# Constants of VectorE's comparisons read from PSUM instead of SBUF, in three layers of a graph network

## The reference

```python
h = relu(layernorm(x)); x = x + L0(h)   # relational: sum over edges of h[src] @ weight[type], 16 types
h = relu(layernorm(x)); x = x + L1(h)   # mean: elu(mean over edges of h[src] @ W_l.T + b_l + h @ W_r.T)
h = relu(layernorm(x)); x = x + L2(h)   # message: m = silu([h[src], h[dst], edge_attr] @ w1 + b1) @ w2 + b2,
                                        #   agg = segment_sum(m, dst), update, layernorm
h = relu(layernorm(x)); x = x + L3(h)   # rule: attention with a softmax per destination and rule, 8 types
# the gather and the sum, as in L1:
msg = x[src]
agg = jax.ops.segment_sum(msg, dst, num_segments=n)
```

## Time and profile before

| | us |
|---|---|
| median of 3 runs | 2359.71 (2354.27 to 2363.16) |
| the profiled execution | 2357.4 |
| its span | 2355.6 |
| POOL busy | 1660.1 (70%) |
| PE busy | 1527.0 (65%) |
| DVE busy | 1062.7 (45%) |
| ACT busy | 486.8 (21%) |

### The profile page before, as it was taken

One profiled execution on the slowest core, in us unless ns is written; L12 is line 12 of the kernel. 1 busy time (PEld: TensorE's weight loads), 2 busy tenths in 40 slices (PEclk: granted clock), 3 DMA queues, 4 the chain that ended last, 5 costly groups with the idle time before them and its releaser, 6 DMA issues.

```text
span 2355.6 us, 28036 instructions
## 1 busy us (share of the span) xinstructions
PE 1527.0 (65%) x8443; PEld 1363.2 (58%) x8443; DVE 1062.7 (45%) x2213; ACT 486.8 (21%) x1153; POOL 1660.1 (70%) x1677
## 2 busy tenths in 40 slices
PE   7573333333588888764887777877858656657774
PEld 3243223322488888764777777777745436646673
DVE  6691111111587666643422222222255765455587
ACT  4000000000098676611100000000032121111120
POOL 5777777777388877872677777777517777777760
PEclk9775555555587777765755555555576886656677
DMA  8613131222111111110322232222217322323220
GB/s 280 205 28 94 24 95 32 68 41 50 25 35 40 35 36 39 38 23 10 79 58 57 58 62 59 57 58 57 44 52 254 84 72 80 77 63 86 68 68 14
DMA packets 159863, 159.27 MB, mean 68 GB/s; under 512 B 108361, under 2 KB 111993, under 8 KB 158748
## 3 DMA queue, kind: packets, MB, share of 16 engines
q0 software_dynamic: 48352, 68.42, 13.4%
q1 hardware_dynamic: 111372, 89.07, 13.3%
HBM read 118.71 MB, written 46.06 MB: 70 GB/s over the span
## 4 chain that ended last, share of the span: by engine, by line
POOL 67%; issue 19%; PE 6%; DVE 4%; DMA 4%; SPq 1%; ACT 0%; POOLq 0%; DVEq 0%; ACTq 0%
POOL flat L591 62%; POOL quiet L579 4%; DMA table<-flat 2%; PE ps L1404 1%; PE ps L1357 1%; PE ps L1657 1%; DMA flat<-table,flat 1%; PE ps L1332 1%; PE ps L1341 1%; PE ps L1601 0%; PE ps L1369 0%; DVE var L681 0%; DVE uvT L674 0%; DVE mean L672 0%; PE ps L1527 0%
## 5 line engine op out<-in xcount | busy, mean ns | idle before, releaser
L591 POOL DMA_INDIRECT flat<-table,flat x1061 | 1146.5, 1081 | 405.0 <-issue 289.1
L1404 PE MATMUL ps<-flat,oh 128*128 x1664 | 323.5, 375 | 393.4 <-DMA flat<-table,flat 367.5
L1404 PEld LDWEIGHTS ps<-flat,oh 128*128 128x128 f32 x1664 | 307.1, 285 | 420.0 <-issue 418.2
L801 DVE TENSOR_TENSOR oh<-iota_n,drel 128x1024 f32<-128x1024 f32 x156 | 190.9, 1224 | 624.7 <-PE ps L1404 424.7
L591 POOL DMA_INDIRECT flat<-table,tile_idx x359 | 348.5, 971 | 111.1 <-issue 94.2
L1369 PE MATMUL ps<-msg,oh 128*128 128x64 f32 x832 | 189.1, 421 | 121.2 <-ACT msg L1225 121.2
L1369 PEld LDWEIGHTS ps<-msg,oh 128*128 128x128 f32 x832 | 179.8, 328 | 129.7 <-issue 129.7
L1382 PE MATMUL ps<-uvT,flat 128*128 128x192 bf16 x2200 | 220.9, 271 | 17.2 <-ACT flat L1207 16.9
L1382 PEld LDWEIGHTS ps<-uvT,flat 128*128 128x128 bf16 x2200 | 215.2, 110 | 22.2 <-issue 17.5
L1527 PEld LDWEIGHTS ps<-uvT,ohT 128*128 128x128 f32 x832 | 191.0, 315 | 17.6
L840 DVE TENSOR_TENSOR flat<-flat,iota_node 128x1536 bf16<-128x1536 f32 x110 | 193.3, 1758 | 3.0
(11 more groups left out here) (321 smaller groups left out, 1514.7 us busy)
## 6 DMA issues: line engine op xcount, KB each, us to landing
table<-flat SPq DMA_DIRECT2D x52, 512.0 KB, 4.9
drow<-slot_node SPq DMA_DIRECT2D x104, 256.0 KB, 3.4
flat<-table,flat POOLq DMA_INDIRECT x1061
flat<-edge_attr_by_slot SPq DMA_DIRECT2D x52, 128.0 KB, 3.7
edge_attr_padded<-edge_attr SPq DMA_DIRECT2D x1, 6250.0 KB
flat<-table,tile_idx POOLq DMA_INDIRECT x359
flat<-tile_source SPq DMA_DIRECT2D x22, 256.0 KB, 3.3
edge_attr_by_slot<-flat SPq DMA_DIRECT2D x2, 2048.0 KB, 6.7
```

What stands on the lines that cost most here:

```text
L591: nc.gpsimd.indirect_dma_start(dest(t % PLACES), None, table, at_).then_inc(tile_gat[k % TRING], 16)
L801: V.tensor_tensor(oh[:, b], iota_n[:].unsqueeze(1).broadcast_to([P, SG, P]), drel[:, g * SG:(g + 1) * SG].unsqueeze(2).broadcast_to([P, SG ...
L1404: last = T.matmul(acc[:, bass.ds(n[j] * pitch + shift, width)], oh[:, b % 2, j, :], got[:, bass.ds(place[j], width)], start=False, stop=Tr ...
```

## The change

Numbers that VectorE compares with are copied into PSUM by matmuls with the identity matrix, and the comparisons read them there.
- Relational layer: at its step 12 TensorE puts `iota_n` into bank 5; one-hots from group OWN = 14 on read it.
- Mean layer: `iota_n` and `iota_node` go into bank 6; all one-hots and all node comparisons of the layer read them. The picked product has one buffer (banks 4 and 5) instead of two, so that pick(q) waits for picked(q-1) instead of picked(q-2).
- Message layer: `iota_n` and `iota_p` go into bank 5 (spare2); the one-hots read the one, and the transposed one-hots, now a two-input comparison, the other. The attribute transposes have one bank (tp[0]) instead of two, so that the transposes of g+2 wait for ScalarE's copy of g+1 instead of g.
- The rule layer keeps the old form.

```diff
--- before.py
+++ after.py
@@ -303,8 +303,12 @@
         assert ASIDE <= WIDE - W and all(room_of(n) // 512 == (room_of(n) + WIDE - 1) // 512 for n in range(NT))
         qr_ps = [ps[:, 2048 + 1024 * k:2048 + 1024 * (k + 1)].rearrange("p (q s c) -> p q s c", q=2, s=4) for k in range(2)]
         assert QR <= P
-        picked_ps = [aux[:, 1024 * q:1024 * q + 256 * PICK].rearrange("p (k c) -> p k c", k=PICK)[:, :, 0:3 * D].rearrange("p k (a d) -> p k a d", a=3)
-                     for q in range(2)]
+        picked_ps = aux[:, 0:256 * PICK].rearrange("p (k c) -> p k c", k=PICK)[:, :, 0:3 * D].rearrange("p k (a d) -> p k a d", a=3)
+        assert 256 * PICK <= 1024
+        columns_ps = (ps[:, 2560:2560 + P], aux[:, 1024:1024 + P])
+        nodes_ps = aux[:, 1024 + P:1024 + P + NT]
+        spare2 = tp[1]
+        OWN = WHOLE[0] + 2
         room = [ps[:, 2048 + 512 * k:2048 + 512 * (k + 1)] for k in range(4)]
 
         def tiles(x):
@@ -796,15 +800,18 @@
                 link(V.memset(carry_f[:], -BIG))
                 link(V.memset(carry_b[:], -BIG))
 
-            def onehots(g, b):
-
-                V.tensor_tensor(oh[:, b], iota_n[:].unsqueeze(1).broadcast_to([P, SG, P]), drel[:, g * SG:(g + 1) * SG].unsqueeze(2).broadcast_to([P, SG, P]),
+            def onehots(g, b, columns=iota_n):
+
+                V.tensor_tensor(oh[:, b], columns[:].unsqueeze(1).broadcast_to([P, SG, P]), drel[:, g * SG:(g + 1) * SG].unsqueeze(2).broadcast_to([P, SG, P]),
                                 ALU.is_equal).then_inc(s("oh"), 1)
 
             def onehots_T(k, g, b):
 
                 dve.wait_ge(drows[b], (k * G // 2 + 1) * 16 + (g - b) * 8)
-                V.tensor_scalar(ohT[:, b], drow[:, b], iota_p[:, 0:1], None, ALU.is_equal).then_inc(s("ohT"), 1)
+                if k == 0:
+                    V.tensor_tensor(ohT[:, b], drow[:, b], spare2[:, P:P + 1].unsqueeze(2).broadcast_to([P, SG, P]), ALU.is_equal).then_inc(s("ohT"), 1)
+                else:
+                    V.tensor_scalar(ohT[:, b], drow[:, b], iota_p[:, 0:1], None, ALU.is_equal).then_inc(s("ohT"), 1)
 
 
             def of_type0(k):
@@ -827,7 +834,9 @@
                 of_type0(0)
                 for g in range(G):
                     dve.wait_ge(s("used"), g + 1)
-                    onehots(g, g % 2)
+                    if g == OWN:
+                        dve.wait_ge(s("numbers"), 1)
+                    onehots(g, g % 2, columns_ps[0] if g >= OWN else iota_n)
                     if g + 1 < WHOLE[0]:
                         of_type0(g + 1)
 
@@ -838,26 +847,27 @@
                     m = TN // CH * q + c
                     dve.wait_ge(s("src_used"), m + 1)
                     V.tensor_tensor(src_oh[:, m % BINS, 0:ON_DVE, :], src_row[:, b].unsqueeze(1).broadcast_to([P, ON_DVE, PICK * P]),
-                                    iota_node[:, CH * c:CH * c + ON_DVE].unsqueeze(2).broadcast_to([P, ON_DVE, PICK * P]), ALU.is_equal).then_inc(s("src_oh"), 1)
+                                    nodes_ps[:, CH * c:CH * c + ON_DVE].unsqueeze(2).broadcast_to([P, ON_DVE, PICK * P]), ALU.is_equal).then_inc(s("src_oh"), 1)
                     dve.wait_ge(s("src_oh"), TN // CH * q + c + 1)
 
-            def picked(q, b):
+            def picked(q):
 
                 dve.wait_ge(s("src_used"), BINS + TN // CH * (q + 1))
                 first = ((q + 1) * 2 * SG + 2 * SG - PICK) % PLACES
-                V.tensor_reduce(got0[:, first:first + PICK, 0:D], picked_ps[b].rearrange("p k a d -> p k d a"), AX, ALU.add).then_inc(s("picked"), 1)
+                V.tensor_reduce(got0[:, first:first + PICK, 0:D], picked_ps.rearrange("p k a d -> p k d a"), AX, ALU.add).then_inc(s("picked"), 1)
 
             def mean_layer():
+                dve.wait_ge(s("numbers"), 2)
                 for i in range(G // 2):
                     q = i
                     if q < PICKS:
                         sources(q, q % 2)
                     dve.wait_ge(s("used"), G + 2 * i + 1)
-                    onehots(2 * i, 0)
+                    onehots(2 * i, 0, columns_ps[1])
                     if q < PICKS:
-                        picked(q, q % 2)
+                        picked(q)
                     dve.wait_ge(s("used"), G + 2 * i + 2)
-                    onehots(2 * i + 1, 1)
+                    onehots(2 * i + 1, 1, columns_ps[1])
 
             segment_bounds()
             dve.sem_inc(s("ohT"), 2)
@@ -963,7 +973,7 @@
                 dve.wait_ge(s("eb_ps"), g + 1)
                 onehots_T(0, g, b)
                 dve.wait_ge(s("used"), 2 * G + g + 1)
-                onehots(g, b)
+                onehots(g, b, spare2[:, 0:P])
 
             def step2(g, b, left):
                 if left > 1:
@@ -977,6 +987,7 @@
                 last.then_inc(s("edge_sum"), 1)
 
             dve.sem_inc(s("edge_sum"), 1)
+            dve.wait_ge(s("numbers"), 3)
             before2(0, 0)
             groups(dve, step2)
             dve.wait_ge(s("used"), 2 + 3 * G)
@@ -1216,7 +1227,7 @@
             def take_ea(g, b):
                 act.wait_ge(s("eaT_ps"), g + 3)
                 act.wait_ge(s("eb_ps"), g + 1)
-                A.copy(eaT[:, b % 2], tp[b % 2][:, 0:2 * P].rearrange("p (q k) -> p q k", q=2)).then_inc(s("eaT_sb"), 1)
+                A.copy(eaT[:, b % 2], tp[0][:, 0:2 * P].rearrange("p (q k) -> p q k", q=2)).then_inc(s("eaT_sb"), 1)
 
             def step2(g, b, left):
                 if left > 2:
@@ -1369,9 +1380,9 @@
                     last = T.matmul(acc[:, bass.ds(n[j] * D, D)], oh[:, b, j, :], rows_[:, j, :], start=False, stop=True, skip_group_check=True)
                 last.then_inc(s("used"), 1)
 
-            def pick(q, b):
-
-                pe.wait_ge(s("picked"), q + 1)
+            def pick(q):
+
+                pe.wait_ge(s("picked"), q + 2)
                 for c in range(TN // CH):
                     m = TN // CH * q + c
                     pe.wait_ge(s("src_oh"), m + 1)
@@ -1379,7 +1390,7 @@
                     for k in range(CH):
                         t = CH * c + k
                         for j in range(PICK):
-                            last = T.matmul(picked_ps[b][:, j], src_oh[:, m % BINS, k, j * P:(j + 1) * P], h_parts[:, :, t, :],
+                            last = T.matmul(picked_ps[:, j], src_oh[:, m % BINS, k, j * P:(j + 1) * P], h_parts[:, :, t, :],
                                             start=(t == 0 and j % 2 == 0), stop=(t == TN - 1), skip_group_check=True)
                     last.then_inc(s("src_used"), 1)
 
@@ -1388,9 +1399,12 @@
 
                 def step(g, b, left):
                     if l == 1 and g % 2 == 0 and g // 2 < PICKS:
-                        pick(g // 2, g // 2 % 2)
+                        pick(g // 2)
                     if l == 0 and g + 1 < WHOLE[0]:
                         typed0(g + 1)
+                    if l == 0 and g == WHOLE[0]:
+                        pe.wait_ge(s("ahead_read"), 4 * WHOLE[0] + 1)
+                        T.matmul(columns_ps[0], ident[:], iota_n[:], start=True, stop=True).then_inc(s("numbers"), 1)
                     n = slot_tiles(PE_, g)
                     place = slot_places(PE_, g)
                     pe.wait_ge(s("oh"), l * G + g + 1)
@@ -1497,6 +1511,8 @@
             pe.wait_ge(s("prep"), 3)
             node_products(aux, hT, pair("wr"))
             pe.wait_ge(s("qn"), 1)
+            T.matmul(columns_ps[1], ident[:], iota_n[:], start=True, stop=True)
+            T.matmul(nodes_ps, ident[:], iota_node[:], start=True, stop=True).then_inc(s("numbers"), 1)
             gathered_sums(1)
             node_transposes(u, *both("u", 1))
             node_products(acc, uT, pair("wl"))
@@ -1515,7 +1531,7 @@
             def ea_T(g, b):
                 pe.wait_ge(eas[b % 2], 16 + (g - b % 2) * 8)
                 for q in range(2):
-                    last = T.transpose(tp[b % 2][:, q * P:(q + 1) * P], ea[:, b % 2, q * P:(q + 1) * P], ident[:])
+                    last = T.transpose(tp[0][:, q * P:(q + 1) * P], ea[:, b % 2, q * P:(q + 1) * P], ident[:])
                 last.then_inc(s("eaT_ps"), 1)
 
             def edges2(g, b, n):
@@ -1534,7 +1550,7 @@
                 if left > 1:
                     n_next = tiles_of[g + 1] = slot_tiles(PE_, g + 1)
                 if left > 2:
-                    pe.wait_ge(s("eaT_sb"), g + 1)
+                    pe.wait_ge(s("eaT_sb"), g + 2)
                     ea_T(g + 2, b + 2)
                 if left > 1:
                     pe.wait_ge(s("edge_sum"), g + 1)
@@ -1543,7 +1559,10 @@
                 pe.wait_ge(s("silu"), g + 1)
                 sum_into_nodes(b % 2, n, msg[:, b % 2])
 
+            T.matmul(spare2[:, 0:P], ident[:], iota_n[:], start=True, stop=True)
+            T.matmul(spare2[:, P:P + 1], ident[:], iota_p[:], start=True, stop=True).then_inc(s("numbers"), 1)
             ea_T(0, 0)
+            pe.wait_ge(s("eaT_sb"), 1)
             ea_T(1, 1)
             edges2(0, 0, tiles_of[0])
```

## The result

The changed kernel takes **2227.51 us** (median of 4 runs, 2225.91 to 2228.14), the one before 2361.43 (median of 4, 2354.27 to 2363.92): ratio 0.9437, 95% interval 0.9414 to 0.9459. The forecast was 2229.

What follows compares the result with a forecast made beforehand. GpSimd's fetches, held up by VectorE comparisons with two SBUF inputs, were taken as the bound: 21.9 + 0.6 + 65.0 + 45.0 - 1.4 = 131.1 us off 2357.4, plus 0.8, gives 2227.1; as median 2229, range 2219 to 2262.

Steps and rivals of the forecast that it cites:

- the signs: Relational, mean and message layers' fetches end about 23, 88 and 132 us earlier; mean fetch falls to about 950 ns.
- The length is the number of fetches times what one takes: All four layers: GpSimd's fetches set the length, at 940 ns least, 945 median, up to 2620 each.
- 21.9 + 0.6: Relational layer: 21.9 us excess of 261 fetches over 945 ns, plus an estimated 0.6 for the first changed group.
- 65.0: Mean layer: 284 fetches averaging 1174 ns against the median 945, so 65.0 us to gain.
- Rival (a): Mean layer becomes TensorE's: 18 us lost, to 2247, or up to 2262 with part of the reduction uncovered; chance 0.11.
- GpSimd's 15.4: Mean layer: GpSimd's time for two groups and a pick after the change, 15.4 us against 18.8 before.
- The prediction's two ends for TensorE: Mean layer, TensorE's cycle: 13.07 us without waits, 16.2 when its sums have slowed after a wait for a fetch.
- 45.0 - 1.4: Message layer: 45.0 us excess of 388 fetches, less 1.4 for the longest, which also meets line 960.
- 0.8 was set for the matmuls: Before the message layer: two identity matmuls and a delayed transpose; 0.8 us taken for all, bounds 0 and 4.
- 318 operations: Comparisons reading PSUM: at some 0.065 us more each by the skill's table, 21 us of VectorE; the sum stays.
- (b): Fetch isn't freed, since any VectorE input or the write holds it: some 2360 us; chance 0.04.
- (c): Numbers repeated 128 or 512 times from PSUM cost two cycles an element: line 840 3.39 us, some 2391; chance 0.03.

Runs made afterwards that it cites:

- the pair of added comparisons: Changed kernel plus one more one-hot comparison per group of the message layer: reading iota_n from SBUF 2260.4 us, reading PSUM instead 2224.82 us.

## Why the prediction was right

**The sum.** Forecast were 131.1 - 0.8 = 130.3 us off the profiled execution, measured are 129.3: 20.4 + 64.9 + 44.1 of the three layers, 0.8 of the rule layer, for which there was no term, less 0.9 in a gap. The layers' last fetches end 20.4, 85.3 and 128.5 us earlier, where the signs said 23, 88 and 132. The mechanism and each layer's size were right; that the median came within 1.5 us of 2229 is closer than runs of one kernel agree with each other (2354 to 2364 before), and to that extent luck: 2.1 us too much was forecast for the relational layer, and 0.5 and 0.8 too little for the message and the rule layer.

**The bound.** "The length is the number of fetches times what one takes" held: the gaps stayed at 383 us, and all of the gain is in the fetches' durations.

**Relational layer.** The sum had 21.9 + 0.6 = 22.5; the layer gained 20.4. From the single fetches, by what they take over 945 ns: those from the 106th on (from 217 us on before) had 21.8 us together and now have none, the eight ahead of them had 0.8 and have none, so 22.6, where the sum had 22.5. The first 97, whose one-hots nothing changes, had 5.7 before and have 8.1 now, and 6.5 in the kernel with this layer on SBUF: they scatter from run to run (5.2 to 8.4 in the profiles that leave these one-hots alone), and the sum has no term for that.

**Mean layer.** 65.0 against 64.9, and it was right by a thin margin. Rival (a), that TensorE takes the layer over, had a basis: between 640 and 960 us picks follow one another every 14.6 us (the third pick starts at 663.05, the last, the 22nd, at 940.79: 277.74 / 19), against GpSimd's 15.4. The prediction's two ends for TensorE were 13.07 and 16.2; the truth lies between, 0.8 under the bound. GpSimd's own cycle, from one clearing of line 583 to the next, is 15.47 to 15.50 us in each of the 21 with 12 fetches that follow the first, so nothing held it up. But TensorE's single cycles run from 13.3 to 15.2 us (one, with a wait for a fetch of 2.64, 16.5): in its slow ones it is only 0.3 under the bound. TensorE's waits in that stretch of the changed kernel (us, times, longest) and the totals of the stretch (its length, then busy PE, PEld, DVE, ACT, POOL, granted clock, share of DMA):

```profile
PE ps L1418 <- DMA flat<-table,flat: 4.6, 2, 2.6
...
PE ps L1418 <- DVE oh L805: 12.2, 20, 0.7
```

```profile
640.00:960.00 320.00, 297.71 (x2844) 288.00 (x2844) 257.26 (x173) 263.42 (x425) 245.11 (x270) 0.88 0.20 43
```

Only two waits for a fetch, PE busy 93% of the stretch, and GpSimd waits for line 1418 three times in the whole span, 0.9 us in all; at 0.3 each these are no longer than its usual gap. The granted clock is 0.88, where the same stretch had 0.80 before. TensorE had fewer waits for fetches than before and the clock was nearer its upper level of 2.4 GHz. With that, 28 of the 43 sums of a group in the stretch took 2.0 us and one 3.67, where from 640 to 1020 us before 13 of 41 took 3.67. That the fewer waits raised the clock and the clock the sums is likely, but no run here separates them. A second gain of this size in the fetches would find TensorE in the way.

**Message layer.** 45.0 - 1.4 = 43.6 against 44.1. The long fetch at its start, 2620 ns, is 2259 now, still under the operation that keeps both inputs in SBUF (line 960 before, 970 now):

```profile
1051.95 1.88 DVE L970 TENSOR_TENSOR xs<-xs,rows 128x1664 f32<-128x1664 f32 x1
...
1052.39 2.26 POOL L595 DMA_INDIRECT flat<-table,flat  x1 [0.30 <-issue]
```

It keeps 1.3 of its 1.7 us over 945 ns, so taking 1.4 back was right. Of the rest, 41.4 us were the one-hots' and 2.5 the transposed ones', by the single records of the kernel before. The prediction's mechanism names only comparisons with two inputs in SBUF; that the scalar form of the transposed ones held fetches too, it had inside its 45.0 without saying so.

**The gaps between layers.** GpSimd waited 51.98 us before the message layer's first fetch, 51.11 before: 0.9 more, where 0.8 was set for the matmuls. Before the mean layer it is 31.22 in both.

```profile
600.91 0.96 POOL L595 DMA_INDIRECT flat<-table,flat  x1 [31.22 <-DMA table<-h]
...
1048.64 0.94 POOL L595 DMA_INDIRECT flat<-table,flat  x1 [51.98 <-DMA table<-uvT]
```

**The forms and the single buffers.** One-hots 1223 ns (forecast 1224), transposed ones 1208 (1230), five node comparisons 8.89 us (8.92). By the cost table of the Trainium skill, "VectorE: DVE Perf Modes", section on the TRN2 errata, they would be an estimated 65 ns longer from PSUM (62 cycles at its 0.96 GHz); the rows show none of it. The prediction counts 318 operations for this; with the first 14 one-hots left on SBUF they are 142 + 110 + 52 = 304, which changes no term of the sum. The single buffers cost nothing, by the kernel with everything else put back (ratio 1.0002).

**Rivals (b) and (c)** fell by the pair of added comparisons and by the row of line 849 (1752 ns, where (c) had 3.39 us). The two doubled one-hots in (c) rested on a misreading: the number that they repeat 128 times is the one in SBUF, not the one from PSUM.

## What to carry to other kernels

Where GpSimd's indirect fetches set the pace, look in the timeline for those longer than their minimum and read what VectorE runs as they start: if it has two SBUF inputs, move the constant one into an idle PSUM bank, which costs one identity matmul. Where no bank is free, cut the operation up: a fetch waits only for the piece that runs as it starts. After that, compute the next engine's cycle before a further step, since here TensorE stood 0.8 us under the bound on average and 0.3 in its slow cycles.

## What the runs showed of the hardware

**The hold has a fixed end.** A fetch that starts under an operation with two SBUF inputs ends 0.81 to 0.83 us after that operation's end, for operations of 0.69 to 1.89 us (one of them, at 625.96 in the changed kernel, was then held again by the cast of line 934, and ended 0.12 after that). From the timeline of the changed kernel, one that still has both inputs in SBUF:

```profile
617.54 1.89 DVE L926 TENSOR_TENSOR flat<-cnt,flat 128x1664 f32<-128x1664 f32 x1
617.62 2.63 POOL L595 DMA_INDIRECT flat<-table,flat  x1 [0.30 <-issue]
```

617.62 + 2.63 = 620.25 is 0.82 after 617.54 + 1.89 = 619.43. A free fetch takes 0.945, so some 0.12 us of it pass before the hold and 0.82 after.

**Who starts first matters, to hundredths of a microsecond.** A fetch that began 0.06 us before the operation ran at its full pace. By the single records of all kept traces the border lies a little ahead of the fetch: two-input comparisons that began 0.045 us or more before it held it, and those that began less than 0.03 us before it, or in its course (369 cases, no fetch over 0.96 us), did not. The Trainium skill, "SBUF — State Buffer", section "SBUF: two separate sides", has this as an exclusive lock that goes to whichever starts first, for the whole instruction. The rows agree with that for a fetch's start, to within those 0.04 us. They don't show the other half of it: one-hots from SBUF that began 0.05 us or more into a fetch took 1.20 to 1.23 us, as always, and the five begun earlier in one at most 1.25. They add that the next of two operations back to back doesn't get in before the waiting fetch (line 840 one after the other, about one fetch in each).

**A late hold of the scalar form.** Begun 0.37 us into a fetch, it stretched it to 0.12 after its own end, and so did all 40 begun from 0.10 to 0.44 us. Two-input comparisons from SBUF have no such late hold: 59 of them began 0.09 to 0.44 us into a fetch and outlasted it, and none of these fetches took over 0.95 us. The same section speaks of a block until VectorE's end and some 115 ns, which fits this case; for a fetch held at its start the rows show 0.82. No run here shows why the two differ.

**Cost by phase.** The scalar form of 0.74 us cost the message layer 2.2 us for 52 operations, and two of them in a row 12.1: what such an operation costs depends on where in the fetches' rhythm it falls, and a small shift elsewhere can change it.
